# One attention-and-experts kernel: the order inside its slots re-planned, and the division by the softmax sum moved into the float16 split

## The reference

```
q, k, v  = layernorm(x) @ Wq, ctx @ Wk, ctx @ Wv     (q and k rms-normalised per head, with weights)
probs    = softmax(q k^T / sqrt(128))                 (over the 128 context tokens)
x        = x + (probs v) @ Wo
logits   = layernorm(x) @ gate^T ; the top 2 of 12, at most `cap` tokens for an expert, in order of token
x        = x + sum over the chosen experts e: w_e * (silu((xs @ w1_e^T) * (xs @ w3_e^T)) @ w2_e^T)
```

## Time and profile before

| | before |
|---|---|
| median of 3 runs | 2715.0 us (2709.59 to 2715.43) |
| the profiled execution | 2715.45 us, its span 2713.7 us |
| busy in the span | PE 2468.4, DVE 1932.4, ACT 1776.6, POOL 1032.3 us |
| mean granted TensorE clock | 0.964 of full speed |

### The profile page before, as it was taken

One profiled execution on the slowest core, in us unless ns is written; L12 is line 12 of the kernel. 1 busy time (PEld: TensorE's weight loads), 2 busy tenths in 40 slices (PEclk: granted clock), 3 DMA queues, 4 the chain that ended last, 5 costly groups with the idle time before them and its releaser, 6 DMA issues. The chain is left out here.

```text
span 2713.7 us, 52797 instructions
## 1 busy us (share of the span) xinstructions
PE 2468.4 (91%) x12889; PEld 1854.0 (68%) x12889; DVE 1932.4 (71%) x5222; ACT 1776.6 (65%) x6581; POOL 1032.3 (38%) x1279
## 2 busy tenths in 40 slices
PE   6799999999999999999999999999999999839983
PEld 4677777777777777777777777777777777625541
DVE  5677777777777777777777777777777777626662
ACT  4677676767677777767676767676776767514541
POOL 2233333333333333333333333333333333247885
PEclk9999999999999999999999999999999999958885
DMA  6455555555555554555555555555555555448997
GB/s 205 106 123 118 118 116 110 116 119 117 116 120 120 116 114 112 118 116 120 116 116 122 114 112 113 121 115 117 120 118 118 117 110 112 98 111 172 189 176 96
DMA packets 768403, 331.20 MB, mean 122 GB/s; under 512 B 694860, under 2 KB 695116, under 8 KB 768336
## 3 DMA queue, kind: packets, MB, share of 16 engines
q1 hardware_dynamic: 743152, 283.41, 46.6%
q0 software_dynamic: 22912, 43.16, 9.0%
q10 hardware_dynamic: 2304, 4.24, 0.5%
HBM read 108.15 MB, written 57.71 MB: 61 GB/s over the span
## 5 line engine op out<-in xcount | busy, mean ns | idle before, releaser
L909 ACT ACTIVATE work<-pb,small 128x128 f32<-128x128 f32 x1024 | 455.1, 455 | 552.7 <-DVE small L1064 552.7
L1079 DVE TENSOR_TENSOR work<-work 128x512 f16<-128x512 f32 x256 | 259.7, 1015 | 281.0 <-ACT work L917 281.0
L802 PE MATMUL pb<-wo_hi,ot_hi 128*128 128x512 f32 x1024 | 418.0, 408 | 18.0 <-DVE ot_lo L1006 10.7
L730 PE MATMUL pb<-wq_hi,x_hi 128*128 128x512 f32 x1024 | 410.9, 401 | 5.2 <-DVE work L1052 5.1
L802 PE MATMUL pb<-wo_hi,ot_lo 128*128 128x512 f32 x1024 | 400.7, 391 | 0.0
L730 PE MATMUL pb<-wq_lo,x_hi 128*128 128x512 f32 x1024 | 400.0, 391 | 0.0
L802 PE MATMUL pb<-wo_lo,ot_hi 128*128 128x512 f32 x1024 | 400.0, 391 | 0.0
L730 PE MATMUL pb<-wq_hi,x_lo 128*128 128x512 f32 x1024 | 399.6, 390 | 0.0
L1052 DVE SCALAR_TENSOR_TENSOR work<-pb,small,work 128x128 f16<-128x128 f32 x1024 | 286.8, 340 | 54.7 <-ACT work L899 54.6
L1329 POOL TENSOR_TENSOR small<-small 128x4 f32<-128x4 f32 x256 | 107.5, 420 | 551.9 <-ACT pb L890 551.9
L899 ACT ACTIVATE work<-pb,small 128x128 f16<-128x128 f32 x1024 | 291.4, 371 | 8.5 <-DMA work<-work 8.4
(11 more groups left out here) (144 smaller groups left out, 5176.1 us busy)
## 6 DMA issues: line engine op xcount, KB each, us to landing
work<-x SPq DMA_DIRECT2D x128, 256.0 KB, 3.2
work<-cT SPq DMA_DIRECT2D x64, 256.0 KB, 2.8
work<-xT SPq DMA_DIRECT2D x64, 256.0 KB, 3.2
out<-work SPq DMA_DIRECT2D x64, 256.0 KB, 4.4
xn_scratch<-work SPq DMA_DIRECT2D x64, 256.0 KB, 2.1
work<-work SPq DMA_TRANSPOSE x640, 3.2
wq_raw<-wq SPq DMA_DIRECT2D x4, 1024.0 KB, 14.2
wo_raw<-wo ACTq DMA_DIRECT2D x4, 1024.0 KB, 6.9
```

What stands on the lines that cost most here:

```text
L730: mm = nc.tensor.matmul(bank[:, :], lhs[a][:, c, :], rhs[b_][:, c, :], start=(c == 0 and n == 0), stop=(c == NC - 1 and n == 2))
L802: mm = nc.tensor.matmul(WO_B[:, :], otp[a][:, h, :], wop[b_][:, g * HPG + h, :], start=(g == 0 and h == 0 and n == 0), stop=(g == NG - 1 a ...
L909: ex = nc.scalar.activation(probs[:, cols], S_B[:, cols], ACT.Exp, bias=nmax[:, h:h + 1], scale=esc, accum_out=psums[:, h:h + 1])
L1079: nc.vector.tensor_tensor(p16[:, LO, :], probs.rearrange("p (h t) -> p h t", h=HPG), p16[:, HI, :], ALU.subtract).then_inc(p_lo, 1)
```

## The change

It does three things.

The normalisation no longer writes the probabilities. `normalise` makes only the four factors `p_rec` = 16384 / sum (a reciprocal and a tensor_scalar on 128x4). ScalarE's high part is made from the unnormalised exponentials in four instructions, one per head, that multiply by the head's factor; DVE's low part likewise in four instructions that multiply and subtract.

The order inside the slots is another one on PE, DVE, ACT, POOL and SP: `route` and `positions`, and with them `copy_logits`, `choose`, `count`, come one slot earlier, `place` comes at the end of g = 3 rather than of the next g = 0, `sum_k` moves in front of the normalisation, `norm2` to the end of its slot; `square_q`, `split_x` come behind the splits of p and q on ScalarE.

At the start the value weights are split ahead of the first query weights, and `fill_tables` is issued with the weight loads, not in batch 1.

```diff
-            LOTS = [("k", 0), ("q", 0), ("v", 0), ("q", 1), ("q", 2), ("q", 3)] + ...
+            LOTS = [("k", 0), ("v", 0), ("q", 0), ("q", 1), ("q", 2), ("q", 3)] + ...
 # SyncE
+                fill_tables()                       (ahead of the loop)
+                        if g == 0 and live(b - 2):
+                            turn_xn2(b - 2)         (was behind turn_p)
+                        if live(b):
+                            turn_p(*cur)
                         if g == 3 and live(b - 1):
                             store_xn2(b - 1)
-                        if live(b):
-                            turn_p(*cur)
-                        if g == 1 and isinstance(b, int) and b == 1:
-                            fill_tables()
 # TensorE
                     if g == 0:
                         wait(pe, v_lo, b + 1)
+                        wait(pe, lg_cp, b - 1)
                     if g == 1:
-                        wait(pe, lg_cp, b - 1)
-                    if g == 2:
                         wait(pe, pm, b - 1)
...
+                        if g == 1 and live(b - 2):
+                            route(b - 2)
                         if g == 2 and live(b - 2):
-                            route(b - 2)
-                        if g == 3 and live(b - 2):
                             positions(b - 2)
 # ScalarE
-                    nc.scalar.copy(p16[:, HI, :], probs.rearrange("p (h t) -> p h t", h=HPG)).then_inc(p_hi, 1)
+                    for h in range(HPG):
+                        hi = nc.scalar.activation(p16[:, h, :], probs[:, h * 128:(h + 1) * 128], ACT.Copy,
+                                                  scale=p_rec[:, h:h + 1])
+                    hi.then_inc(p_hi, 1)
...
-                        if live(far[0]):
-                            square_q(*far)
-                        if g == 0 and live(b + 1):
-                            split_x(b + 1)
                         if g == 3 and live(b + 2):
                             split_c(b + 2)
                         if live(b):
                             split_p(*cur)
                         if live(near[0]):
                             split_q(*near)
+                        if live(far[0]):
+                            square_q(*far)
+                        if g == 0 and live(b + 1):
+                            split_x(b + 1)
 # VectorE
-                    nc.vector.scalar_tensor_tensor(out=pv, in0=pv, scalar=PS,
-                                                   in1=rsums[:, :, None].broadcast_to([128, HPG, 128]),
-                                                   op0=ALU.mult, op1=ALU.mult).then_inc(p_nrm, 1)
+                    wait(dve, p_hi, u)
+                    nc.vector.tensor_scalar(p_rec, rsums, PS, None, ALU.mult).then_inc(p_nrm, 1)
...
-                    nc.vector.tensor_tensor(p16[:, LO, :], probs.rearrange("p (h t) -> p h t", h=HPG), p16[:, HI, :],
-                                            ALU.subtract).then_inc(p_lo, 1)
+                    for h in range(HPG):
+                        lo = nc.vector.scalar_tensor_tensor(
+                            out=p16[:, 4 + h, :], in0=probs[:, h * 128:(h + 1) * 128], scalar=p_rec[:, h:h + 1],
+                            in1=p16[:, h, :], op0=ALU.mult, op1=ALU.subtract)
+                    lo.then_inc(p_lo, 1)
 # GpSimd
-                        if g == 1 and live(b - 3):
+                        if g == 0 and live(b - 3):
                             scatter(b - 3)
```

More of the change, by code:

```diff
@@ L501, in sm @@
                 return v if dt is f32 else v.bitcast(dt)
-            smax, nmax, psums, rsums = sm(4), sm(4), sm(4), sm(4)
+            smax, nmax, psums, rsums, p_rec = sm(4), sm(4), sm(4), sm(4), sm(4)
             q_ssq, q_ms, q_rms = sm(4), sm(4), [sm(4), sm(4)]
@@ L554, in build @@
             block = ctx.enter_context(nc.Block())
-            LOTS = [("k", 0), ("q", 0), ("v", 0), ("q", 1), ("q", 2), ("q", 3)] + [("o", n) for n in range(NG)]
+            LOTS = [("k", 0), ("v", 0), ("q", 0), ("q", 1), ("q", 2), ("q", 3)] + [("o", n) for n in range(NG)]
             SPLIT_FIRST = {(-1, 1): (1, 2, 3), (-1, 2): (4,), (-1, 3): (5,)}
             SPLIT_LAST = {(0, 1): (6,), (0, 2): (7,), (0, 3): (8,), (1, 0): (9,)}
-            MEANS = {(-1, 0): (1,), (-1, 1): (3,), (-1, 2): (4,), (-1, 3): (5,)}
+            MEANS = {(-1, 0): (2,), (-1, 1): (3,), (-1, 2): (4,), (-1, 3): (5,)}
             def lots(table, b, g):
@@ L672, in _ @@
                 load_stat(0)
-                for l in range(1, 6):
+                for l in (2, 1, 3, 4, 5):
                     load_lot(l)
@@ L676, in _ @@
                 sp.wait_ge(s_const, 1)
+                fill_tables()
                 def body(b):
@@ L686, in body @@
                             load_c(b + 2)
+                        if g == 0 and live(b - 2):
+                            turn_xn2(b - 2)
                         if g == 1 and live(b - 1):
@@ L695, in body @@
                             turn_k(b + 1)
+                        if live(b):
+                            turn_p(*cur)
                         if g == 3 and live(b - 1):
                             store_xn2(b - 1)
-                        if live(b):
-                            turn_p(*cur)
-                        if g == 0 and live(b - 2):
-                            turn_xn2(b - 2)
-                        if g == 1 and isinstance(b, int) and b == 1:
-                            fill_tables()
                 loop(sp, body)
@@ L808, in route @@
                     wait(pe, d_xT, 16 * (b + 1))
-                    wait(pe, ot_lo, min(4 * b + 9, NU) if isinstance(b, int) else 4 * b + 9)
+                    wait(pe, ot_lo, min(4 * b + 8, NU) if isinstance(b, int) else 4 * b + 8)
                     for c in range(NC):
@@ L818, in positions @@
                     wait(pe, mac, b + 1)
-                    wait(pe, ot_lo, min(4 * b + 10, NU) if isinstance(b, int) else 4 * b + 10)
+                    wait(pe, ot_lo, min(4 * b + 9, NU) if isinstance(b, int) else 4 * b + 9)
                     nc.tensor.matmul(OT_B[:, 0:2 * E], tri[:, :], mask, start=True, stop=False)
@@ L975, in body @@
                             split_v(b)
+                        if g == 2 and live(b - 2):
+                            exp_diff(b - 2)
                         if g == 3 and live(b + 1):
@@ L1244, in body @@
                             split_v(b)
+                        if g == 2 and live(b + 1):
+                            sum_k(b + 1)
                         if g == 3 and live(b + 1):
                             split_k(b + 1)
-                        if g == 3 and live(b - 1):
-                            norm2(b - 1)
                         if live(b):
@@ L1252, in body @@
                             widen_p(*before)
-                        if g == 2 and live(b - 2):
-                            copy_logits(b - 2)
-                        if g == 3 and live(b - 2):
-                            count(b - 2)
                         if live(b):
                             split_p(*cur)
+                        if g == 1 and live(b - 2):
+                            copy_logits(b - 2)
+                        if g == 2 and live(b - 2):
+                            count(b - 2)
                         if live(near[0]):
@@ L1262, in body @@
                             stats_x(b + 1)
-                        if g == 0 and live(b - 3):
-                            place(b - 3)
-                        if g == 1 and live(b + 1):
-                            sum_k(b + 1)
+                        if g == 1 and live(b - 2):
+                            choose(b - 2)
                         if g == 2 and live(b + 1):
                             norm_k(b + 1)
-                        if g == 2 and live(b - 2):
-                            choose(b - 2)
                         if g == 2 and live(b - 1):
                             stats_2(b - 1)
+                        if g == 3 and live(b - 1):
+                            norm2(b - 1)
+                        if g == 3 and live(b - 2):
+                            place(b - 2)
                         for l in lots(SPLIT_LAST, b, g):
@@ L1357, in body @@
                             split_c(b + 2)
+                        if g == 2 and live(b + 1):
+                            rms_k(b + 1)
                         if live(far[0]):
@@ L1361, in body @@
                             eps_of_x(b + 1)
-                        if g == 1 and isinstance(b, int) and b == 2:
+                        if g == 0 and isinstance(b, int) and b == 2:
                             pool.wait_ge(d_sent, 32)
-                        if g == 1 and live(b - 3):
+                        if g == 0 and live(b - 3):
                             scatter(b - 3)
-                        if g == 1 and live(b + 1):
-                            rms_k(b + 1)
                         if g == 2 and live(b - 1):
```

3 lines of the change are left out of this document (removed).

## The result

| | before | after |
|---|---|---|
| median, us | 2714.7 (4 runs, 2709.6 to 2715.4) | 2597.9 (4 runs, 2593.7 to 2602.5) |
| ratio, 95% interval | | 0.9574 [0.9552, 0.9596] |
| profiled execution, us | 2715.45 | 2595.63 |
| its span, us | 2713.7 | 2593.7 |
| one batch, us | 36.0 | 34.3 |

The account below looks back on a forecast made before the run. The DVE–ScalarE ring was taken to bound the kernel, not PE: 2715.45 − 152.5 (61 batches, 36.0 to 33.5 us) − 4.3 (batches 0 and 1) − 6.3 (`fill_tables`) = 2552 us; range 2515 to 2640.

Parts of the forecast that it names:

- The bound: In the batch loop, a DVE to ScalarE to DVE cycle, not PE, sets the 36.0 us period.
- the stretch: Each slot from DVE's reciprocal to `split_q`: its start was to come 0.54 us earlier, 2.16 for four slots.
- the ring: Maxima, exponentials, splits and back to maxima over four slots: 36.0 us a batch before, 33.5 after.
- PE's floor: PE's own work in a batch: four slots of 8.20 plus gate logits and positions, 33.05 us.
- Rival (a): In the loop, cheaper pieces let PE set the period: 2525 us; chance 0.76 together with forecast and (d).
- The pieces of p: Four-piece splits of p from SBUF, taken like `split_q`'s: 1.14 us on ScalarE, 1.04 on DVE.
- the small operations: `copy_logits` and `count` now stand between the two splits on DVE: +0.3 us a batch.
- The collision with GpSimd's low parts: GpSimd's low parts of x and context lengthen DVE's low part of p, 1.34 for 0.69 us; taken as unchanged, 0.
- (d): x's low part 0.5 us late for PE's queries in g = 1: 2583 us; chance 0.76 with forecast and (a).
- (b): GpSimd's moved `scatter` and low part of x hold up DVE in g = 1, +1.95 a batch: 2671 us; chance 0.10.
- (c): The 32 small SBUF pieces a batch are dear, up to 39.3 us a batch and 2905 us; chance 0.14.
- Context's low part: Comes well before the next slot's keys, so PE's wait of 24.2 us in all is gone.

Follow-up runs that it names:

- order_only: The changed kernel with the old normalisation (one product over 512 columns, one cast, one subtraction), new order kept: 2552.2 us, 0.9404 against the kernel before.
- order_x_place: order_only with the cast of x ahead of the squares in g = 0 and `place` ahead of `norm2`: 2547.0 us, 0.9393 against the kernel before.
- x_first_place: The changed kernel with the cast of x ahead of the squares in g = 0 and `place` ahead of `norm2`: 2572.1 us, 0.9471 against the kernel before.
- before_act_order: The kernel before with only ScalarE's queue changed, squares and cast of x behind the splits of p and q: 2583.9 us, 0.9527.

## Why the prediction was right, and where its size was off

*The bound.* Right. The batch was a ring between DVE and ScalarE with PE below it: one edit of ScalarE's queue alone, with no work saved, gives 128 us, and undoing it takes all of the gain. Of the 3.37 us that this edit took out of the stretch, 2.05 a batch were gained; the rest came back as a collision and a wait elsewhere on the ring.

*PE's floor.* 33.05 us was too low. In `order_only`, with PE nearly without a wait (5.5 us in all from 120 to 2200 us), the batch is 33.5, and in `order_x_place`, where the maxima wait for PE in every second slot, the same. PE's weight loads show the slots by the start of the scores:

```profile
1206.90 0.67 PEld L773 LDWEIGHTS pb<-work 128*128 128x128 f16 x12 [0.26 <-issue]
...
1215.50 0.67 PEld L773 LDWEIGHTS pb<-work 128*128 128x128 f16 x12 [0.26 <-issue]
...
1223.91 0.67 PEld L773 LDWEIGHTS pb<-work 128*128 128x128 f16 x12 [0.26 <-issue]
...
1232.16 0.67 PEld L773 LDWEIGHTS pb<-work 128*128 128x128 f16 x12 [0.26 <-issue]
...
1240.42 0.67 PEld L773 LDWEIGHTS pb<-work 128*128 128x128 f16 x12 [0.26 <-issue]
```

8.60, 8.41, 8.25 and 8.26 us. A plain slot is 8.25, not the 8.20 read from one stretch, and the gate logits and the positions add 0.35 and 0.16, more than the matmuls counted for them. Rival (a) could therefore not have come much below the 2547 us of `order_x_place`.

*The ring, −2.5 forecast, −1.7 measured.* This is the step that was mis-sized. By the table of the slots the forecast comes to 11.86 for the stretch (14.29 − 2.43) and 21.65 for the rest (21.71 − 0.06). Measured were 11.99 and 22.30. The terms of the stretch:

- The pieces of p (taken 1.14 on ScalarE, 1.04 on DVE). Measured: 1.28 on ScalarE, 1.19 from the first copy to q's first, and 1.06 on DVE. The copies from SBUF are slower than `split_q`'s from PSUM, though the whole cast from either showed only 0.018 between them. DVE's part starts 1.31 behind the copies' start (1.18 taken). The plain stretch is 2.79, without the small operations of `copy_logits` and `count`, where 2.64 was forecast, 0.15 more; in g = 3 it is 0.18 more and in g = 0 0.23: +0.7 a batch, the largest single error. Of the 0.54 a slot that I gave to the squares' move and p's split in four together, 0.55 was the squares'. I never priced the fold against the one-piece form in the new order, which would have been 0.16 to 0.41 a slot shorter.
- The collision with GpSimd's low parts, taken as unchanged. It is gone: p's four pieces last 1.14 in all slots. In g = 3 GpSimd's low part of the context (1222.07 to 1223.35) is all but over when they start at 1223.21. Its cost before is what 14.29 has above four plain slots of 3.18 and two casts of 0.51: −0.55.

Together with the small operations (0.27 for 0.3) these two leave 0.13. That the stretch came out so near its forecast is luck: two errors of half a microsecond and more cancelled. The rest of the batch is 0.65 longer than forecast:

- The loop's end on DVE, not in the sum: +0.41. In `x_first_place` 0.36 a batch went with it.
- `choose` takes 1.04 in the changed kernel's g = 1, 0.19 more than before, 0.21 of it a wait of its match load. In `order_only`, where it stands in the same place, it takes 0.94, so its new place isn't the whole reason; the reason stays open.

```profile
1207.59 0.17 DVE L1126 MAX8 small<-small 128x8 f32<-128x12 f32 x1
1207.96 0.09 DVE L1128 MATCH_VALUE_LOAD small<-small 128x8 f32 x1 [0.21 <-DVE small L1126]
```

- `norm2` cost 0.45 (0.54 taken), −0.09. Some 0.14 are left in small differences.

0.13 + 0.41 + 0.19 − 0.09 + 0.14 is 0.78, from 33.51 to the 34.29 measured. Only the loop's end and the fold as a whole were tested by runs of their own; the split of the rest is read from the traces.

*The rivals.* (d), the late x, came as described, but beside the ring and not on top of it: 31.5 us of waiting were worth 5 at most. (b), GpSimd in DVE's way, left no trace in the changed kernel: in g = 1, beside the first DMA_INDIRECT of `scatter` (1203.57), `p_rec` at 1203.87 lasts 0.17 as elsewhere, and the cast of `widen_p` lasts 428 ns in the mean. But the argument against it, that operations of a few columns read almost nothing, doesn't always hold: in `before_act_order` one of two columns was held up by GpSimd's low part of x for 0.54. (c), dear pieces, is where the largest single error went, at a small size: about 0.04 a copy on ScalarE, next to nothing on DVE. The estimate of 1.16 for DVE's four was worked out from a formula that the Trainium skill, VectorE: DVE Perf Modes, section The TRN2 errata — SBUF-src ops pay a fixed extra latency per instruction, gives for a float32 addition of two tensors. From start to next start the four took 1.06, and 1.14 from the first's start to the last's end. What was dear stood on ScalarE.

*The small terms.* Context's low part: its wait of 24.2 us is gone, as said. `fill_tables`: 6.3 forecast, 8 to 11 measured by its own run, and nothing lost at the start. PE's waits for `copy_logits` and `count` stayed at or below 0.4 us. The starting order of the weight splits wasn't tried alone, and neither were the moves on PE, SP and GpSimd.

## What to carry to other kernels

Where no engine is full, follow the work around one slot until it comes back to where it began, and write down what stands in that ring; work of another slot that merely waits in the same queue inside it (here four squares of 1.13 us) can cost time in every slot (here 0.55, the rest being covered by DVE's product), and moving it was worth more here than the rewriting. Price a fusion by what it adds on the ring, not by the work it removes: the product folded away here had been hidden beside the squares, and folding it cost 143 us in the old order and 46 in the new. Look also at what a move brings side by side on two other engines: part of this gain was a collision with GpSimd that went away, which the forecast had left as it was. A wait that the trace shows may run beside the ring and be worth nothing; only the ring's own length, taken over several slots, says so.

## What the runs showed of the hardware

- ScalarE's scaled copies of 128 columns to float16, four in a row: 1.28 us from SBUF (395 ns each in the mean), 1.11 to 1.14 from PSUM (358 to 371 ns in the kernels here), while one cast of 512 columns from SBUF to float16 took 0.62. Splitting a cast into four costs 0.66 us here.
- A DVE instruction that runs beside one of GpSimd's low parts (128x512, two inputs) can be held up, even a small one: p's low part of 512 columns lasted 1.34 to 1.37 us for 0.69, and in `before_act_order` a `place` operation of 2 columns 0.69 for 0.15 and `count`'s sum of 24 columns 1.17 for 0.16. Four other small ones beside that same low part of x kept their 0.15 to 0.18.
- The end of a loop's body shows on an engine that gets there with short instructions queued: 0.41 us of idleness on DVE behind `place`'s small operations (58 times), none behind a 512-column one. The Trainium skill, Advanced Engine Details and Errata, section Control Flow Timing, gives 51 to 108 ns for a branch; the trace shows several times that where nothing covers it.
- The untouched experts' part differed by up to 10 us between profiled executions (329.8 to 340.0), as much as the smaller edits are worth; the residuals' distance inside the loop tells such edits apart better than the total.
